# A transformer block: the shared expert's down products as three 16-bit products each, with the weights' ranges measured earlier

## The reference

```python
x = x + attention(cond_attention(x))
h = mixer(x)                                     # layer norm at its end
# in the feed-forward, on h (2048 tokens x 256)
probs = softmax(rms_norm(h) @ router_w.T); best two experts, capacity 320 each
eout  = (silu(xg @ rg[e]) * (xg @ ru[e])) @ rd[e]     # per expert, I = 1024
shared = silu(h @ sg) * (h @ su) @ sd                 # I = 2048
x = x + shared + routed
```

## Time and profile before

| | |
|---|---|
| median of 3 runs | 1601.72 us (1598.1 to 1601.99) |
| the profiled execution | 1594.84 us, span of its instructions 1593.0 us |
| busy | PE 91%, DVE 65%, ACT 51%, POOL 42% of the span |
| mean granted clock of PE | 0.958 of full speed |
| attention stage | to about 1027 us |
| shared chunks 0 to 2 | about 1027 to 1310 us |
| experts | about 1310 to 1503 us |
| shared chunk 3 and the sums | about 1503 to 1593 us |

### The profile page before, as it was taken

One profiled execution on the slowest core, in us unless ns is written; L12 is line 12 of the kernel. 1 busy time (PEld: TensorE's weight loads), 2 busy tenths in 40 slices (PEclk: granted clock), 3 DMA queues, 4 the chain that ended last, 5 costly groups with the idle time before them and its releaser, 6 DMA issues. The chain is left out here.

```text
span 1593.0 us, 21701 instructions
## 1 busy us (share of the span) xinstructions
PE 1455.9 (91%) x7649; PEld 693.1 (44%) x7697; DVE 1032.9 (65%) x2506; ACT 810.3 (51%) x975; POOL 666.1 (42%) x455
## 2 busy tenths in 40 slices
PE   4788999999999999888998878799999999999988
PEld 2513333332433332333343323345566567777745
DVE  8789878889767886665877493554451437667232
ACT  3753666787556666457765657733332134334101
POOL 5336799998769999613312012141000300000160
PEclk9759999999999999999999979799999999999999
DMA  2340010231311111113242022130000223544061
GB/s 80 122 132 9 27 41 29 89 80 56 80 34 47 38 39 27 35 35 83 91 115 74 21 71 71 55 101 3 1 0 24 93 70 111 177 153 135 28 121 28
DMA packets 74759, 104.52 MB, mean 66 GB/s; under 512 B 14843, under 2 KB 49092, under 8 KB 74650
## 3 DMA queue, kind: packets, MB, share of 16 engines
q1 hardware_dynamic: 70730, 96.66, 20.1%
q0 software_dynamic: 3072, 6.03, 1.9%
q10 hardware_dynamic: 848, 0.43, 0.1%
HBM read 72.39 MB, written 32.77 MB: 66 GB/s over the span
## 5 line engine op out<-in xcount | busy, mean ns | idle before, releaser
L1475 ACT ACTIVATE sb_prob<-wide,sb_ranges 128x1024 f32<-128x1024 f32 (+3 forms) x384 | 380.1, 1006 | 207.8 <-PE wide L2218 114.5
L1249 POOL TENSOR_TENSOR sb_prob<-sb_prob,sb_weight 128x1024 f32<-128x1024 f32 x192 | 448.9, 2363 | 73.1 <-ACT sb_prob L1475 70.9
L2213 PE MATMUL wide<-sb_stack_q,sb_stack_k 114*128 114x512 f16 (+3 forms) x896 | 282.4, 364 | 15.6 <-ACT sb_prob L1475 7.7
L1799 DVE CUSTOM_DVE_ANT_0 sb_junk<-bank,sb_bias 128x512 bf16<-128x512 f32 x345 | 230.4, 687 | 54.0 <-PE bank L2183 49.2
L1522 ACT ACTIVATE sb_sil<-wide,sb_weight 128x320 f32<-128x320 f32 (+1 forms) x128 | 77.5, 607 | 316.0 <-PE wide L2299 259.1
L2183 PE MATMUL bank<-sb_stack_k,sb_stack_q 112*128 112x512 f16 (+3 forms) x601 | 217.2, 378 | 20.5 <-DVE sb_rowmax L1799 5.7
L2233 PE MATMUL wide<-sb_prob,sb_v_aug 128*17 128x512 f32 (+3 forms) x1792 | 223.6, 564 | 10.3 <-ACT sb_o_raw L1487 8.8
L2299 PE MATMUL wide<-sb_weight,sb_ffn 128*128 128x512 f16 x768 | 181.4, 388 | 9.2 <-DVE sb_act_s L2012 7.3
L2012 DVE SCALAR_TENSOR_TENSOR sb_act_s<-wide,sb_weight,sb_sil 128x512 f32<-128x512 f32 x64 | 47.9, 749 | 186.8 <-ACT sb_sil L1522 172.8
L1254 POOL TENSOR_SCALAR_AFFINE_SELECT sb_prob<-sb_prob 128x256 f32<-128x256 f32 x128 | 53.0, 420 | 244.6 <-ACT sb_prob L1475 244.5
L2183 PEld LDWEIGHTS bank<-sb_stack_k,sb_stack_q 112*128 112x128 f16 x601 | 58.8, 98 | 205.4 <-issue 91.3
(11 more groups left out here) (311 smaller groups left out, 1921.2 us busy)
## 6 DMA issues: line engine op xcount, KB each, us to landing
o_raw<-sb_o_raw SPq DMA_DIRECT2D x32, 256.0 KB, 2.2
sb_weight<-rg SPq DMA_DIRECT2D x8, 1024.0 KB, 4.8
sb_xT<-ru SPq DMA_DIRECT2D x8, 1024.0 KB, 4.8
sb_big<-rd SPq DMA_DIRECT2D x8, 1024.0 KB, 6.2
parts<-sb_o_norm SPq DMA_DIRECT2D x40, 128.0 KB
sb_stack_q<-parts SPq DMA_DIRECT2D x32, 128.0 KB, 3.2
sb_stack_k<-parts SPq DMA_DIRECT2D x32, 128.0 KB, 3.2
sb_o_norm<-o_raw SPq DMA_DIRECT2D x64, 64.0 KB, 2.2
```

The source lines that it names most:

```text
L1249: e.tensor_tensor(p, p, weight_of(*u[1:]), ALU.mult).then_inc(weigh_p.handle, 1)
L1475: e.activation(p[:, :, first:HALF], sc[:, :, first:HALF], ACT.Exp, scale=unscale).then_inc(SC.empty_sem(u), 1)
L1799: e.tensor_tensor_reduce(out=junk[:, i % 2, 0:hi - lo], in0=BK.tile(u)[:, 0:hi - lo], in1=bias[:, qt, lo:hi], scale=1.0, scalar=-3e38, op0 ...
L2213: i = e.matmul(sc[:, j * HALF + first:(j + 1) * HALF], stack_k[0:ROWS_M, n % 3, pair, kt * P:(kt + 1) * P], stack_q[0:ROWS_M, n % 3, PAIRS ...
```

## The change

Every down product of the shared half is made like gate and up: `sd` and the activations are split in two 16-bit parts, and three part products are added in PSUM. A column's down goes from 4 fp32 matmuls to 12 16-bit ones.

- **Activations** (`ahigh`, `alow`): VectorE's product of silu and up goes into `sil`, in place. ScalarE then copies it to fp16 (`ahigh`), and VectorE subtracts that from it into a bf16 low part (`alow`). Both lie in the `act_s` buffer. `alow` of column i stands in the list behind `gu` of column i + 1, and the down product of i, at its old place, waits for it. ScalarE's silu of column i waits for `alow` of i - 2, which frees its `sil` buffer.
- **One scale for all blocks** of a weight: the maxima of `sg`, `su` and `sd` (`MEASURES`, 3 x 4) are taken in advance from loads of their own (512 KB each, three buffers in `room_after`), three in each of jobs 10 to 13 (`measure_steps`). One `wsum` ("p") at the start of job 14 makes all scales, gains, the down weights' scale and the factors that undo them, in 15 small dependent operations of VectorE.
- **Splits**: no `wabs` or `wsum` of a block is left in jobs 14 and 15 or in chunk 0. `EARLY_AT`, `BLOCK_COLUMNS` and `DOWN_COLUMNS` place the splits: in job 14 gate, up and down of block 0; in job 15 gate and up of block 1; in chunk 0 block 2 in columns 2 and 3, block 3 in 6 and 7, and the down weights of blocks 1, 2 and 3 in columns 3, 6 and 9. The raw down weights are loaded by units of their own (`ffndown`), of blocks 1 to 3 into a part of `e_out`, as two DMAs each.
- **Undoing the scale**: the residual's identity is scaled by one factor (`ident_down`), and the copies and sums at a chunk's end multiply by the inverse.

```diff
-EARLY_AT = (0.05, 0.25, 0.35, 0.5, 0.6, 0.75)
-BLOCK_COLUMNS = {2: (1, 2, 3, 3, 4), 3: (7, 8, 9, 9, 10)}
+EARLY_AT = (0.03, 0.4, 0.5, 0.52, 0.92)
+EARLY_DOWNS = 1
+BLOCK_COLUMNS = {2: (2, 3), 3: (6, 7)}
+DOWN_COLUMNS = {1: 3, 2: 6, 3: 9}
...
+def split_steps(k):
+    return [("wsplit", "s", k, z) for z in range(SHARED_PARTS)]
+
+def measure_steps(opened, k):
+    each = MEASURES // MEASURE_JOBS
+    out = [(opened, 2, j, ("measure_load", j)) for j in range(MEASURE_SLOTS)] if k == 0 else []
+    for i, j in enumerate(range(k * each, (k + 1) * each)):
+        at = opened + (1 - opened) * (i + 1.5) / (each + 1)
+        out.append((at, 3, 2 * j, ("wabs", "p", j, 0)))
+        if j + MEASURE_SLOTS < MEASURES:
+            out.append((at, 3, 2 * j + 1, ("measure_load", j + MEASURE_SLOTS)))
+    return out
...
 def early_weights(opened, k):
-    steps = [("ffnload", k), *weight_steps("s", k)]
+    if k == 0:
+        out.append((opened + 0.02, 2, len(out), ("wsum", "p", 0)))
+    gate, up, down = split_steps(k)
+    steps = [("ffnload", k), gate, up] + ([("ffndown", k), down] if k < EARLY_DOWNS else [])
...
 def shared_plan(tc, others, at=None):
     for i in range(COLUMNS_S):
+        if i:
+            plan.append(("ahigh", tc, i - 1))
         plan.append(("gu", "s", tc, i))
+        if i:
+            plan.append(("alow", tc, i - 1))
         plan += at.get(i, []) if at else []
         if i >= DOWN_LAG:
             plan.append(("down", "s", tc, i - DOWN_LAG))
...
+    plan += [("ahigh", tc, COLUMNS_S - 1), ("alow", tc, COLUMNS_S - 1)]
     plan += [("down", "s", tc, i) for i in range(COLUMNS_S - DOWN_LAG, COLUMNS_S - 1)]
...
@@ SyncE
+            def load_down(k):
+                w.wait_ge(low_d.after(("wsplit", "s", k, 0) if k < EARLY_DOWNS else ("wsplit", "s", k - 1, 2)))
...
+                elif kind == "measure_load":
+                    j = u[1]
+                    if j >= MEASURE_SLOTS:
+                        w.wait_ge(abs_d.after(("wabs", "p", j - MEASURE_SLOTS, 0)))
+                    e.dma_start(raw_of("p", j, 0), shared_rows(j % BLOCKS, j // BLOCKS)
+                                ).then_inc(measure_in[j % MEASURE_SLOTS].handle, 16)
...
@@ ScalarE
-                        w.wait_ge(SC.emptied(GUS[i - 2]))
+                        w.wait_ge(act_low_d.after(GUS[i - 2]) if GUS[i - 2][1] == "s" else SC.emptied(GUS[i - 2]))
...
+                elif kind == "ahigh":
+                    key_ = ("gu", "s", *u[1:])
+                    if SHARED[key_] >= 3:
+                        w.wait_ge(down_done(*GUS_S[SHARED[key_] - 3][1:]))
+                    w.wait_ge(SC.emptied(key_))
+                    e.activation(act_parts(key_)[0], sil[:, GU[key_] % 2, 0:HALF], ACT.Copy).then_inc(act_high_a.handle, 1)
...
@@ VectorE
-                        dst = act_s[:, SHARED[u] % 3]
-                        if SHARED[u] >= 3:
-                            w.wait_ge(down_done(*GUS_S[SHARED[u] - 3][1:]))
+                        dst = sil[:, j % 2, 0:n]
...
+                elif kind == "alow":
+                    key_ = ("gu", "s", *u[1:])
+                    high, low = act_parts(key_)
+                    w.wait_ge(act_high_a.after(key_))
+                    e.tensor_tensor(low, sil[:, GU[key_] % 2, 0:HALF], high, ALU.subtract).then_inc(act_low_d.handle, 1)
...
@@ TensorE
-                        w.wait_ge(ffn_in[i // ROWS_B].end)
-                        a = act_s[:, SHARED["gu", "s", x, i] % 3]
+                        w.wait_ge(low_d.after(("wsplit", "s", i // ROWS_B, 2)))
+                        w.wait_ge(act_low_d.after(("gu", "s", x, i)))
+                        a = act_parts(("gu", "s", x, i))
                         final = i == COLUMNS_S - 1
                         for t in range(TPC):
-                            m = e.matmul(acc[:, t * D:(t + 1) * D], a[:, t * P:(t + 1) * P], wsd[i // ROWS_B][:, i % ROWS_B],
-                                         start=(i == 0 and t % 2 == 0), stop=final, skip_group_check=True)
+                            for k, (wp, ap) in enumerate(PAIRED):
+                                m = e.matmul(acc[:, t * D:(t + 1) * D], a[ap][:, t * P:(t + 1) * P],
+                                             wsd16[i // ROWS_B][:, wp, i % ROWS_B],
+                                             start=(i == 0 and t % 2 == 0 and k == 0),
+                                             stop=final and k == len(PAIRED) - 1, skip_group_check=True)
```

More of the change, by code:

```diff
@@ L78 @@
 PAIRED = ((0, 0), (0, 1), (1, 0))
-EARLY_AT = (0.05, 0.25, 0.35, 0.5, 0.6, 0.75)
-BLOCK_COLUMNS = {2: (1, 2, 3, 3, 4), 3: (7, 8, 9, 9, 10)}
+EARLY_AT = (0.03, 0.4, 0.5, 0.52, 0.92)
+EARLY_DOWNS = 1
+BLOCK_COLUMNS = {2: (2, 3), 3: (6, 7)}
+DOWN_COLUMNS = {1: 3, 2: 6, 3: 9}
+SHARED_PARTS = 3
+MEASURES = SHARED_PARTS * BLOCKS
+MEASURE_JOBS, MEASURE_SLOTS = 4, 3
+SHARED_SCALES = ("square", "bounded", "power", "root", "low", "scale", "norm", "inverse", "limit", "act", "back",
+                 "gain", "up", "out", "total")
+SUMS = MEASURES + 2 * BLOCKS
+TOP_DOWN, LIMIT = 2.0 ** 12, 2.0 ** 10
 EXPERT_COLUMNS, FIRST_COLUMNS = (0, 1, 3, 4, 5), (6, 7, 9, 10, 12)
@@ L800, in raw_of, with down_rows, part_of, summed @@
             piece = w_ffn[:, RAW_AT[k][z][0], RAW_AT[k][z][1]] if k < EARLY else fetched[:, z * DC * COLS:(z + 1) * DC * COLS]
             return piece.rearrange("p (c m) -> p c m", c=DC)
+        def down_rows(k, ap):
+            return ap if k < EARLY_DOWNS else ap.rearrange("p (a b) n -> p a b n", a=2)
+        def part_of(name, k, z, part):
+            if name == "s" and z == 2:
+                return down_rows(k, wsd16[k][:, part])
+            return parts_of(name, k, z)[:, part]
+        def summed(name, k):
+            return ("p", 0) if name == "s" else (name, k)
@@ L816, in build, with act_parts @@
+        def act_parts(u):
+            both = act_s[:, SHARED[u] % 3]
+            return both.bitcast(F16)[:, 0:HALF], both.bitcast(BF16)[:, HALF:2 * HALF]
         load = {k: signal(f"load_{k}", range(n), 16) for k, n in dict(
             cb=2, idx=3, ones=6, cf=2, x0=2, x1=2, w1=1, w2=1, wo=1, small=3, mix=13, wproj=1).items()}
-        ffn_in = [signal(f"load_ffn{k}", ["sd"], 16) for k in range(BLOCKS)]
+        measure_in = [signal(f"load_measure{k}", range(k, MEASURES, MEASURE_SLOTS), 16) for k in range(MEASURE_SLOTS)]
@@ L819, in build @@
         raw_in = {(n, z): signal(f"load_raw_{n}{z}", range(BLOCKS if n == "s" else E), 16)
                   for n in ("s", "e") for z in range(2)}
+        down_in = signal("load_raw_down", [(k, a) for k in range(BLOCKS) for a in range(1 if k < EARLY_DOWNS else 2)], 16)
         abs_d = signal("dve_weight_abs", of("wabs"))
-        scale_d = signal("dve_weight_scale", [(u, k) for u in of("wsum") for k in ("power", "low", "scale", "gain")])
+        scale_d = signal("dve_weight_scale", [(u, k) for u in of("wsum") for k in (
+            SHARED_SCALES if u[1] == "p" else ("power", "low", "scale", "gain"))])
@@ L1370, in weight_high @@
                 _, name, k, z = u
-                w.wait_ge(scale_d.after((("wsum", name, k), "scale")))
+                w.wait_ge(scale_d.after((("wsum", *summed(name, k)), "scale")))
+                if name == "s":
+                    w.wait_ge(down_in.after((k, int(k >= EARLY_DOWNS))) if z == 2 else raw_in["s", z].after(k))
                 if name == "e" and k >= 2:
@@ L1528, in _ @@
                     w.wait_ge(sent[tc * HALF // S].end)
+                    w.wait_ge(scale_d.after((("wsum", "p", 0), "out")))
                     for t in range(TPC):
-                        i = e.activation(y[:, tc * TPC + t], acc[:, t * D:(t + 1) * D], ACT.Copy)
+                        i = e.activation(y[:, tc * TPC + t], acc[:, t * D:(t + 1) * D], ACT.Copy, scale=s_down[:, 2:3])
                     i.then_inc(ACC.empty_sem(("acc", "s", tc)), 1)
@@ L2116, in total @@
                 n = 1 if name == "r" else 2
+                if name == "p":
+                    w.wait_ge(abs_d.after(("wabs", "p", MEASURES - 1, 0)))
+                    w.wait_ge(scale_d.after((u, "square")))
+                    w.wait_ge(ring(u).vacant(u))
+                    e.matmul(ring(u).tile(u)[:, 0:SUMS], C["ones"], s_max, start=True, stop=True).then_inc(ring(u).full_sem(u), 1)
+                    return
                 w.wait_ge(abs_d.after(("wabs", name, k, n - 1)))
@@ L2326, in _ @@
                     tc = u[1]
+                    w.wait_ge(ident_d.end)
                     acc = ACC.tile(("acc", "s", tc))
```

127 lines of the change are left out of this document (105 added, 22 removed).

## The result

The changed kernel takes 1612.16 us (median of 5 runs, 1606.57 to 1617.84) beside 1601.41 for the kernel before on the same chip (5 runs, 1596.5 to 1601.99): ratio 1.0098, 95% interval 1.0067 to 1.0129. It is slower; 1597 was forecast and 1608 was the top of the range. The profiled executions are 1606.57 and 1594.84 us, 11.7 apart.

The account below looks back on a forecast made before the run. TensorE was taken to bound most of the shared feed-forward, with VectorE, GpSimd or ScalarE deciding elsewhere. From 1027 us on -7.8 and attention +3 gave -4.8 from 1601.7, so 1597 us; the 8 in 10 range was 1584 to 1608.

Parts of the forecast that it names:

- What comes ahead of that: Attention, before 1027 us: maxima mostly fit in jobs 10 and 11 (+1), later jobs +2.4 and -0.5; together +3 us.
- rival (d): Down products: 16-bit matmuls with a load each do not stream; at 0.216 us each, +56 us, 1657; chance 0.03.
- The wait at a chunk's end: Chunks 1, 2 and 3: the last but one down waits for its subtraction, 1.0 us lost.
- 1100 to 1127: Chunk 0, VectorE full: TensorE waits 1.7 and 2.6 us at downs 9 and 10; 28.1 against 27.0, +1.1 us.
- Chunk 0: 1027 to 1152.9 us: four stretches forecast at +0.4, -0.3, +1.1 and -0.5 us.
- Chunk 1: To 1230.4 us: two downs -0.8, layer norm stretch 0, nine downs -3.8, end +1.0; about 3.5 us shorter.
- Chunk 2: To 1310.3 us: first five downs 0, scatter stall 0 (-2 to +4), eight downs -3.4, end +1.0.
- Chunk 3: From 1503.4 us: GpSimd's gathers decide up to 1555.7 (0), then eight downs -3.4, end +1.0, final sums +0.1.
- All behind attention: Everything from 1027 us on, experts untouched: about -7.8 us in sum.
- (b): Jobs 10 to 15: VectorE's added work is not hidden, attention +11; slower, 1605, or 1607 with ScalarE's upper bound; chance 0.18.
- (a): TensorE bounds nearly everywhere, no waits behind VectorE in chunks 0 to 2, attention unchanged: -20 us, 1582; chance 0.18.
- (c): GpSimd gather stretches: longer instruction stream brings one more stall of 10.7 to 13.5 us; 1603 to 1608; chance 0.12.

Follow-up runs that it names:

- Experiment 1: Changed kernel with the first three loads for the maxima issued one job earlier (job 9, not 10), maxima unmoved; ratio 1.0020 to the kernel before.
- experiment 3: Changed kernel without measurement: the twelve loads and maxima left out, a constant in their place; ratio 0.9991 to the kernel before.
- experiment 4: Changed kernel with the twelve maxima in jobs 8 to 11 and the first loads in job 7; ratio 1.0005 to the kernel before.
- experiment 6: Experiment 1's kernel with job 15's two splits of block 1 at 0.6 and 0.75 of the job, not 0.4 and 0.5; ratio 1.0003.
- experiment 7: Experiment 1's kernel with four maxima in each of jobs 10 to 12 and none in job 13; ratio 1.0031 to the kernel before.
- experiment 8: Experiment 6's kernel with chunk 3's sums spread, one tile's combine per column instead of two; ratio 0.9927 to the kernel before.
- experiment 10: Experiment 8's kernel with splits of block 1 in columns 0 and 1 of chunk 0, block 2's in 3 and 4; ratio 0.9904.
- experiment 9: Kernel before with only chunk 3's sums spread over its columns, down products still fp32; ratio 0.9963 to the unedited kernel before.
- experiment 2: Changed kernel with each maximum over 32 or 64 elements per partition, all loads and waits kept; ratio 1.0051 to the kernel before.
- experiment 5: Kernel before and changed kernel, both unedited, again as a pair on a second chip; 1577.42 us for one run before, ratio 1.0088 for the changed one.

## Why the prediction was wrong

**The step that failed** is the sum under "What comes ahead of that": "In jobs 10 and 11 ... one maximum more mostly fits: +1, between 0 and +5", and of the loads only that the row stores behind them have "microseconds to spare". It priced VectorE's work and asked what the loads delay, not when the first one lands. Attention cost 19.3 us in the profiled pair, against +3. 10.5 of it (10.7 in the second pair) arise in job 10, where a maximum stood in VectorE's in-order queue ahead of its data. Experiment 1 shows it: the same work with its data there costs 11 to 12.5 us less. The size can be estimated once it is asked: three loads of 512 KB together, at the 258 to 276 GB/s of the windows above, land some 6 us after their issue, and the issue came 1.8 us later than VectorE reached the maximum.

**The parts, one by one.**
- Down column 1.31 us and pure column 3.90: as forecast. Matmuls of 110 ns with a weight load each do stream; rival (d) is out.
- The wait at a chunk's end, 1.0 forecast: 0.84 at the end of chunk 3.
- 1100 to 1127: waits of 1.40 and 2.61 us on downs 9 and 10 for 1.7 and 2.6; from the same product to the same product (1119.82 to 1147.95) the stretch is 28.1 long, as forecast.
- Chunk 0: +0.5 for +0.7 (+1.9 on the second chip). Chunk 1: -3.6, as forecast. But once the loads stand earlier or are left out, chunk 0 takes 129.5 to 132.3 us (experiments 1, 3, 4, 6, 7, 8 and 10), with a mean clock of 0.93 to 0.95; the second pair has 125.7 before and 127.6 after, at 0.99 and 0.96. A part of what attention won back is lost again there, and no run shows why. The first five microseconds of the chunk, changed kernel and experiment 6 (clock 1.00 and 0.50):

```profile
1047.80:1052.80 5.00, 4.97 (x66) 2.98 (x67) 0.27 (x2) 1.97 (x2) 0.00 (x0) 1.00 0.80 257
```

```profile
1036.40:1041.40 5.00, 4.96 (x12) 1.75 (x13) 0.18 (x1) 0.00 (x0) 0.00 (x0) 0.50 0.81 275
```

- Chunk 2: -0.1 for -2.4 on the first chip with a stall of 10.59 us in it, -4.2 on the second without. Its sign and range were right; "down 1 waits 1.9 for subtraction 1, which eats the first five downs" was too dear.
- Chunk 3: -4.2 for -2.3 on the first chip, +0.6 on the second. "up to 1555.7 GpSimd's 32 gathers (31.16 us busy) decide: 0" was right; but of the eight downs behind it, -3.4, nothing was seen without the stalls. Experiments 8 and 9 show that the sums' place in VectorE's queue held it. The -4.2 of the first chip stand beside one stall of 12.56 us less than before.
- All behind attention: -7.6 on the first chip, -5.6 on the second, for -7.8 (the forecast's own stretches add up to -7.6). That the first fits so well is luck: it holds one long stall fewer in chunk 3, where the forecast's gain was not there without the stalls.
- Jobs 10 to 13 beyond the late load: 4.6 us in time by experiments 1 and 3, near the upper end of the forecast's 0 to +5. Job 14: +1.0 for +2.4. Job 15 to the first column: +3.0 for -0.5, over its bound of +2; later splits took it away in the trace.

**The rivals.** (b) had the right side and place (slower, by attention) and some of the size, 1605 to 1607 for 1612, but its mechanism, VectorE's work not hidden, is worth about 5 of the 19 us; a late transfer was named by none. (a) is refuted by the waits. (c) is refuted as an effect of the longer program: the changed kernel had two stalls of over 10 us where the kernel before had three (the prediction counted two), and on the second chip neither kernel had one.

**What stays open.** 5.1 us of the 19.3 lie in job 13, where the clock fell in the changed kernel and not in the kernel before; the second pair has the same 5.1. All traces, from the store that opens job 13 to the next one, with 97 matmul records in each (one of the job's three maxima lies in it):

| trace | maxima in job 13 | us | mean clock |
|---|---|---|---|
| kernel before, both chips | none | 29.1 | 1.00 |
| kernel before with spread sums (9) | none | 35.1 | 0.81 |
| changed kernel, both chips | three | 34.2 | 0.85 |
| experiments 1, 6, 8, 10 | three | 35.5 to 35.9 | 0.81 |
| experiment 2 | three small | 30.7 | 0.94 |
| experiment 3 | none | 30.6 | 0.94 |
| experiment 4 | none | 29.9 | 1.00 |
| experiment 7 | none | 35.9 | 0.81 |

The large fall stands in all six traces that have three whole maxima in the job, and in two of the seven others. So it goes with the maxima, but it also comes without them, and how often each kernel pays it was not measured. The cause of these 5 us is not shown.

## What to carry to other kernels

Before a load and its consumer are put into in-order queues, write down two times: when the queue issues the load and it lands (with all that is issued beside it), and when the consumer's engine gets there; a consumer that comes first stops its engine and all who wait for it. A cheaper product shows only where its engine sets the pace: in chunk 3 other work in VectorE's queue, waiting for gathers, had to be moved first, and then 5.5 us appeared of the 6.7 that 16 columns of 0.42 can give. And move work out of a stage only after seeing what the stage's own chain runs through.

## What the runs showed of the hardware

The granted clock can take either level on the same instructions with the same busy times. Job 13 of the kernel before, windows of two executions (experiment 5, and experiment 9, whose attention stage is the same program):

```profile
868.80:875.70 6.90, 5.63 (x30) 1.42 (x30) 6.29 (x23) 2.99 (x8) 1.22 (x3) 1.00 0.78 222
875.70:883.70 8.00, 5.38 (x25) 1.58 (x25) 5.86 (x14) 6.91 (x7) 0.00 (x0) 1.00 0.02 8
883.70:889.70 6.00, 5.53 (x22) 2.04 (x23) 2.21 (x8) 4.30 (x6) 0.00 (x0) 1.00 0.00 0
889.70:897.90 8.20, 8.05 (x21) 3.27 (x21) 0.97 (x2) 2.49 (x5) 0.00 (x0) 1.00 0.00 0
```

```profile
872.10:879.00 6.90, 5.63 (x30) 1.43 (x30) 6.30 (x23) 2.98 (x7) 1.22 (x3) 1.00 0.77 222
879.00:887.00 8.00, 5.38 (x25) 1.58 (x25) 5.86 (x14) 6.90 (x7) 0.00 (x0) 1.00 0.02 7
887.00:893.00 6.00, 5.96 (x18) 2.44 (x19) 2.30 (x8) 2.96 (x3) 0.00 (x0) 0.58 0.00 0
893.00:907.20 14.20, 14.04 (x25) 5.19 (x23) 0.98 (x2) 3.95 (x8) 0.00 (x0) 0.70 0.00 0
```

TensorE is busy for 5.63 of 6.9 and 5.38 of 8.0 us in both; then the clock stays at 2.4 GHz in one and is down at 1.2 GHz for a part of the time in the other (0.58 and 0.70 on the mean), and the rest of the job takes 20.2 instead of 14.2 us. This is a difference of 6 us between two executions of one program, and runs of the kernel before on one chip spread from 1577.5 to 1591.0. The Trainium skill ("TensorE: Matmul & The Clock Gate", section "What's actually happening") calls the number of slow matmuls of one kernel variable from run to run, at a kernel's start; the pair above shows such a difference in its middle.

Job 8 shows it again. Its 240 matmul records are the same in these traces, and no maximum for the weights is in it: it takes 48.0 to 48.5 us at a mean clock of 0.96 in both kernels on both chips and in experiments 1 and 6, 49.6 and 49.8 at 0.93 in experiments 3 and 9, and 52.9 at 0.87 in experiments 2, 7, 8 and 10.

ScalarE's stalls of 10.6 to 13.5 us beside GpSimd's indirect DMAs were in both kernels' traces from the first chip and in no trace from the three others; the kernel before takes 79.9 us for chunk 2 with them and 73.2 without.
